# Two expert layers on one Trainium2 core: loop bodies of four tiles, four buffers of gathered rows, and a token table put in tile order

## The reference, cut to what matters

```python
router_logits = xt @ gate_w.T
routing_weights = jax.nn.softmax(router_logits, axis=-1)
top_w, top_idx = jax.lax.top_k(routing_weights, TOP_K)
full_w = jnp.zeros_like(routing_weights).at[rows, top_idx].set(top_w)
full_w = full_w / jnp.clip(full_w.sum(axis=-1, keepdims=True), 1e-09, None)
g = jax.nn.silu(jnp.einsum('th,ehi->eti', xt, w_gate))
u = jnp.einsum('th,ehi->eti', xt, w_up)
y = jnp.einsum('eti,eih->eth', g * u, w_down)
out = jnp.einsum('eth,te->th', y, full_w)
```

## Time and profile before

| | us |
|---|---|
| median of 3 runs | 1076.29 |
| lowest and highest run | 1075.6, 1079.83 |
| the profiled execution | 1073.37 |
| its span in the trace | 1071.6 |
| PE busy | 811.7 (76%) |
| DVE busy | 515.7 (48%) |
| ACT busy | 524.3 (49%) |
| POOL busy | 499.5 (47%) |
| mean granted TensorE clock | 0.908 |

### The profile page before, as it was taken

The page is one execution under the profiler, slowest core; times in us unless marked ns, Lnnn a source line. Parts: engine busy times, 40 slices in busy tenths (PEclk is TensorE's granted clock), DMA queues, the critical chain, the costliest instruction groups (busy, mean ns, idle before and its releaser), DMA issues.

```text
span 1071.6 us, 20434 instructions
## 1 busy us (share of the span) xinstructions
PE 811.7 (76%) x5206; PEld 441.1 (41%) x5207; DVE 515.7 (48%) x1523; ACT 524.3 (49%) x782; POOL 499.5 (47%) x413
## 2 busy tenths in 40 slices
PE   4998999997389993769871377878877778777770
PEld 3444455544244442335341243444444444444440
DVE  5653444564435533557763243544545435353432
ACT  5532334544356741345452165556756556555550
POOL 4880001001346755004575555566766556656560
PEclk9999999998589996979985698999999999989995
DMA  8553010000348958301110358878987878779668
GB/s 283 168 182 118 11 40 21 31 30 31 111 126 217 236 101 240 129 30 41 41 42 23 108 129 234 194 165 195 242 221 191 228 165 199 186 169 233 150 111 254
DMA packets 108391, 150.73 MB, mean 141 GB/s; under 512 B 18336, under 2 KB 59552, under 8 KB 108352
## 3 DMA queue, kind: packets, MB, share of 16 engines
q0 software_dynamic: 25760, 56.56, 26.9%
q1 hardware_dynamic: 80000, 93.49, 26.6%
q10 hardware_dynamic: 2592, 0.19, 0.2%
HBM read 107.34 MB, written 42.86 MB: 140 GB/s over the span
## 4 chain that ended last, share of the span: by engine, by line
PE 39%; DMA 15%; issue 14%; DVE 10%; DVEq 8%; ACT 5%; SPq 3%; POOL 3%; ACTq 2%; POOLq 0%; another core or an unknown queue 0%
PE pst L187 32%; DMA mid<-moe_normalised_rows,small 6%; DMA big<-in_L_ffn_w_down_dram 4%; DMA x_rows<-mid,small 3%; DVEq L1160 3%; DVEq L1154 2%; PE pst L1264 2%; PE pst L493 2%; POOL moe_tokens_of_experts L994 1%; DVE big L1146 1%; DMA big<-x_rows 1%; ACTq L1154 1%; DVE mid L1385 1%; DMA big<-in_L_ffn_wo_dram 1%; PE pst L953 1%
## 5 line engine op out<-in xcount | busy, mean ns | idle before, releaser
L187 PE MATMUL pst<-big,mid 128*128 (+1 forms) x1392 | 287.0, 359 | 22.1 <-DVE mid L1377 10.4
L1460 POOL DMA_INDIRECT x_rows<-mid,small x100 | 160.1, 1601 | 130.9 <-ACT mid L1321 77.0
L994 POOL DMA_INDIRECT moe_tokens_of_experts<-token_no,small x80 | 82.8, 1035 | 285.4 <-DVE small L1047 264.9
L187 PEld LDWEIGHTS pst<-big,mid 128*128 128x128 f16 x1392 | 137.8, 102 | 137.1 <-issue 47.6
L1450 POOL DMA_INDIRECT mid<-moe_normalised_rows,small x106 | 114.7, 1082 | 97.4 <-DVE small L1367 37.4
L1264 PE MATMUL pst<-big,mid 128*128 x520 | 132.3, 388 | 1.4 <-ACT mid L1313 0.9
L1302 ACT ACTIVATE mid<-pst 128x1024 f16<-128x1024 f16 x102 | 103.7, 1017 | 55.7 <-PE pst L1236 44.0
L1377 DVE SCALAR_TENSOR_TENSOR mid<-pst,small,mid 128x192 f32<-128x192 f32 (+1 forms) x100 | 42.6, 426 | 119.8 <-ACT mid L1308 87.8
L1236 PE MATMUL pst<-id,mid 128*128 128x128 f16 x816 | 66.5, 228 | 39.0 <-DMA mid<-moe_normalised_rows,small 34.5
L187 PE MATMUL pst<-ctxN,mid 128*128 128x512 f16 x384 | 88.6, 389 | 3.2 <-ACT mid L619 3.2
L1321 ACT ACTIVATE mid<-pst 128x512 f32<-128x512 f32 x100 | 59.9, 599 | 58.0 <-PE pst L1264 46.0
(11 more groups left out here) (201 smaller groups left out, 1193.4 us busy)
## 6 DMA issues: line engine op xcount, KB each, us to landing
big<-in_L_ffn_w_gate_dram SPq DMA_DIRECT2D x32, 384.0 KB
big<-in_L_ffn_w_up_dram SPq DMA_DIRECT2D x32, 384.0 KB
big<-in_L_ffn_wi_dram SPq DMA_DIRECT2D x16, 512.0 KB
big<-in_L_ffn_w_down_dram SPq DMA_DIRECT2D x32, 256.0 KB
big<-in_L_ffn_w_down_dram SPq DMA_DIRECT2D x64, 128.0 KB
moe_normalised_rows<-xn SPq DMA_DIRECT2D x18, 256.0 KB, 2.0
mid<-in_ctx_dram SPq DMA_DIRECT2D x16, 256.0 KB, 4.3
big<-in_ctx_turned_dram SPq DMA_DIRECT2D x16, 256.0 KB, 4.6
```

The source lines that it names most:

```text
L187: last = nc.tensor.matmul(dst, stationary(a, c), moving(b, c), start=(k == 0), stop=(k == 3 * len(parts) - 1))
L994: nc.gpsimd.indirect_dma_start(out=self.tab_d[:, :], out_offset=bass.IndirectOffsetOnAxis(ap=self.addr[j % 2][:, k:k + 1], axis=0), in_=to ...
L1460: nc.gpsimd.indirect_dma_start(out=acc_d[p][:, :], out_offset=bass.IndirectOffsetOnAxis(ap=self.si[p], axis=0), in_=self.y[p], in_offset=N ...
```

## The change

The loops take four tiles a turn. `experts` reads its numbers once per four tiles (5 values on DVE, ACT and POOL, 6 on PE), and `columns` is gone. In its place the whole table of row numbers is put in tile order once, before the loop: a 0/1 matrix `sel` has a one where table column c belongs to tile n; DVE casts the table to float16, PE transposes it, DVE copies it, PE multiplies by `sel` and adds the spare rows for tiles past the end, and DVE copies the result to `rows`, where tile t's row numbers are column t+2. There are four buffers `xg` and four index columns `gi`; the extra two buffers lie in `xT`. DVE makes h of t, splits it at once, copies the router weight of t+1, the row numbers of t+5, the rows to add to of t-2, and splits weights for the expert of t+2 last. The constants of the routing are made at the program's start, and the counts start from an earlier semaphore (`m_s` for `key_s`). The low part of the down weights in `moe1` is one subtraction of 128x1024 instead of two.

```diff
             def experts(self, eng, it, first, n):
                 _, values = nc.values_load_multi_w_load_instructions(
-                    self.etab[0:1, bass.ds(2 * it + first + 2, n)], engines=[eng.engine], min_val=0,
+                    self.etab[0:1, bass.ds(4 * it + first + 2, n)], engines=[eng.engine], min_val=0,
...
-            def columns(self, eng, it, first, n):
-                _, values = nc.values_load_multi_w_load_instructions(
-                    self.ctab[0:1, bass.ds(2 * it + first + 2, n)], engines=[eng.engine], min_val=0,
...
-            def dve_pair(self, dve, it, first):
-                e = self.experts(dve, it, 0, 3)
-                c = self.columns(dve, it, -2, 7)
-                for p in range(2):
-                    t = 2 * it + p
-                    self.rows_in_turn(dve, it + 1 + p, t + 3, 1 - p, c[5 + p])
-                    self.weights_in_turn(dve, it + 1 + p, t + 1, 1 - p, e[1 + p])
-                    if not (first and p == 0):
-                        self.h_high(dve, t - 1, 1 - p)
-                        self.h_low(dve, t - 1, 1 - p)
-                    with dve.If(e[p + 1] > e[p]):
-                        self.split_d_lo(dve, e[p + 1])
+            def dve_quad(self, dve, it, first):
+                e = self.experts(dve, it, 1, 5)
+                for q in range(4):
+                    t, p, g = 4 * it + q, q % 2, (q + 1) % 4
                     self.make_h(dve, t, p)
-                    if not first:
-                        self.rows_out(dve, it - 1, t - 2, p, c[p])
+                    self.h_high(dve, t, p)
+                    self.h_low(dve, t, p)
+                    self.weights_in_turn(dve, it + (2 if q == 3 else 1), t + 1, g, e[q])
+                    self.rows_in_turn(dve, t + 5, g)
+                    if not (first and q < 2):
+                        self.rows_out(dve, 2 * it + q // 2 - 1, t - 2, p)
+                    with dve.If(e[q + 1] > e[q]):
+                        self.split_d_lo(dve, e[q + 1])
...
+            def dve_rows(self, dve):
+                NE = self.NE
+                dve.wait_ge(self.tab_in, 32)
+                nc.vector.tensor_copy(self.tab16, self.tab).then_inc(self.rows_s, 1)
+                dve.wait_ge(self.route_pe, 5)
+                nc.vector.tensor_copy(self.tabT[0:self.CQ, :, :], bank16(3)[0:self.CQ, 0:self.NQ * P].rearrange("p (q s) -> p q s", q=self.NQ)).then_inc(self.rows_s, 1)
+                dve.wait_ge(self.route_pe, 6)
+                link(dve, nc.vector.tensor_copy(self.rows, bank(5)[:, 0:NE]))
...
-            def pool_pair(self, pool, it, first):
-                e = self.experts(pool, it, 1, 3)
-                for p in range(2):
-                    t = 2 * it + p
-                    self.gather(pool, t + 3, 1 - p)
+            def pool_quad(self, pool, it, first):
+                e = self.experts(pool, it, 1, 5)
+                for q in range(4):
+                    t, p = 4 * it + q, q % 2
+                    self.gather(pool, t + 5, (q + 1) % 4)
-                    with pool.If(e[p + 1] > e[p]):
-                        self.split_gu_lo(pool, e[p + 1])
+                    with pool.If(e[q + 1] > e[q]):
+                        self.split_gu_lo(pool, e[q + 1])
-                    if not first:
-                        self.scatter(pool, it - 1, t - 2, p)
+                    if not (first and q < 2):
+                        self.scatter(pool, 2 * it + q // 2 - 1, t - 2, p)
```

More of the change, by code:

```diff
@@ L882, in __init__ @@
                 self.r8 = small[:, 38:39]
-                self.gi = [small[:, 58 + q:59 + q].bitcast(I32) for q in range(2)]
+                self.gi = [row_no[:, q:q + 1] for q in range(4)]
                 self.si = [small[:, 60 + q:61 + q].bitcast(I32) for q in range(2)]
@@ L905, in __init__ @@
                 self.si_s = sem(f"{name}_rows_to_add_to")
-                self.xg_in = [sem(f"{name}_rows_gathered_{i}") for i in range(2)]
+                self.xg_in = [sem(f"{name}_rows_gathered_{i}") for i in range(4)]
                 self.x_full = sem(f"{name}_rows_transposed")
@@ L1183, in pe_route @@
             def pe_route(self, pe):
-                E = self.E
-                pe.wait_ge(self.key_s, self.b + NT)
+                E, NE = self.E, self.NE
+                pe.wait_ge(self.m_s, self.b + NT)
                 for t in range(NT):
-                    last = nc.tensor.matmul(bank(5)[0:E, 0:P], self.m16[:, t, :], ones16[:], start=(t == 0), stop=(t == NT - 1))
+                    last = nc.tensor.matmul(bank(4)[0:E, 0:1], self.m16[:, t, :], ones16[:, 0:1], start=(t == 0), stop=(t == NT - 1))
@@ L1189, in pe_route @@
                 last.then_inc(self.route_pe, 1)
                 pe.wait_ge(self.tab_s, 1)
[L1192 to L1194 removed]
+                nc.tensor.matmul(bank(3)[0:1, 12:12 + E], self.nt16, before16[0:E, 0:E], start=True, stop=True)
@@ new lines, in pe_route @@
+                nc.tensor.matmul(bank(4)[0:1, 192:192 + NE], self.nt16, self.past, start=True, stop=True).then_inc(self.route_pe, 1)
+                pe.wait_ge(self.tab_s, 3)
+                nc.tensor.matmul(bank(4)[:, 320:320 + NE], ones16[0:1, :], self.crow, start=True, stop=True).then_inc(self.route_pe, 1)
+                pe.wait_ge(self.rows_s, 1)
+                for q in range(self.NQ):
+                    last = nc.tensor.transpose(bank16(3)[0:self.CQ, q * P:(q + 1) * P], self.tab16[:, q * self.CQ:(q + 1) * self.CQ], id16[:])
@@ L1200, in act_route @@
+                last.then_inc(self.route_pe, 1)
+                pe.wait_ge(self.rows_s, 2)
+                for q in range(self.NQ):
+                    nc.tensor.matmul(bank(5)[:, 0:NE], self.tabT[0:self.CQ, q, :], self.sel[0:self.CQ, q, :], start=(q == 0), stop=False)
+                nc.tensor.matmul(bank(5)[:, 0:NE], spare16[:], self.over, start=False, stop=True).then_inc(self.route_pe, 1)
             def act_route(self, act):
@@ new lines, in dve_route @@
+                nc.vector.tensor_scalar(self.over, passed, E - 0.5, None, ALU.is_ge)
+                link(dve, nc.vector.scalar_tensor_tensor(self.colrow, earlier, -1.0, tile_row[0:1, :], ALU.mult, ALU.add))
+                link(dve, nc.vector.scalar_tensor_tensor(self.colrow, self.colrow, float(E), passed, ALU.mult, ALU.add))
+                nc.vector.scalar_tensor_tensor(self.crow, self.over, 4096.0, self.colrow, ALU.mult, ALU.add).then_inc(self.tab_s, 1)
+                dve.wait_ge(self.route_pe, 4)
@@ new lines, in dve_route @@
+                for q in range(self.NQ):
+                    nc.vector.tensor_scalar(self.sel[:, q, :], b4[:, 320:320 + NE], part_no[:, q:q + 1], None, ALU.is_equal)
+            def dve_rows(self, dve):
[6 more added lines that the diff above has]
+                link(dve, nc.vector.tensor_copy(self.rows, bank(5)[:, 0:NE]))
@@ L1321, in weigh, with act_quad @@
                 nc.scalar.activation(self.y[p], bank(6 + p), ACT.Copy).then_inc(self.y_s, 1)
[L1323 to L1327 removed]
+            def act_quad(self, act, it, first):
+                e = self.experts(act, it, 2, 5)
+                for q in range(4):
+                    t, p = 4 * it + q, q % 2
                     self.move_rows(act, t + 1, 1 - p)
                     self.silu(act, t, p)
[L1330 removed]
+                    if not (first and q == 0):
                         self.move_h(act, t - 1, 1 - p)
[L1332 to L1335 removed]
+                    if not (first and q < 2):
+                        self.weigh(act, 2 * it + q // 2 - 1, t - 2, p)
+                    with act.If(e[q + 1] > e[q]):
+                        self.split_hi(act, e[q + 1], self.first_tile(act, e[q + 1]))
             def act(self, act):
@@ L1446, in gather @@
+                self.dve_quad(dve, 0, True)
+                with dve.Fori(1, nq) as it:
+                    self.dve_quad(dve, it, False)
+                n = 4 * nq
+                self.rows_out(dve, 2 * nq - 1, n - 2, 0)
+                self.rows_out(dve, 2 * nq - 1, n - 1, 1)
+            def gather(self, pool, t, g):
                 pool.wait_ge(self.meta_s, t + 1 + self.CR)
-                pool.wait_ge(self.x_full, t - 1 + self.CR)
-                pool.wait_ge(self.wc_s, t - 1 + self.CR)
+                pool.wait_ge(self.x_full, t - 3 + self.CR)
+                pool.wait_ge(self.wc_s, t - 3 + self.CR)
```

270 lines of the change are left out of this document (123 added, 147 removed).

## The result

The changed kernel is **slower**: 1101.1 us (median of 4 runs, 1100.43 to 1107.07), where the kernel before took 1078.06 beside it (4 runs, 1075.6 to 1081.84). The ratio is 1.0223, 95% interval 1.0173 to 1.0272. The forecast was 1023, and its range ended at 1048.

The account below looks back on a forecast made before the run. The long expert loop was held by late DVE, DMA engines stopping the gain near 4.2 us per tile. Terms -48 - 2 - 4 + 1 = -53 took 1073.4 to 1020, 1023 as a median; range 1004 to 1048.

Parts of the forecast that it names:

- Order on DVE: Long loop: DVE's weight splits move from ahead of h of t to the tile's end; 8 us off.
- Four buffers: Long loop: a gather has four tiles' time to land, not two; 21 of PE's 25.6 us wait off.
- The rival: Scatters into one DRAM sum limit two tiles; long landings make the kernel slower, 1096, as a median 1099; chance 0.03.
- 1.45 + 1.08: Added to a scatter's landing: 1.45 us until the next on its sum, 1.08 for POOL's gather ahead of it.
- Gathers under 5: Sign of being right: PE's wait for gathers in the long loop falls from 26 to under 5 us.
- loads -33: Long loop: fewer register loads on DVE take 33 us off PE's 43.0 us wait before the transposes of h.
- Start of `moe1`: Long stage: first row numbers come 2 us earlier (ends: 4 off, 1 on), table put in tile order included.
- forecast 1 on: Short stage: table steps add 1.8 us, loads of some 0.6 move behind; 1 us on (0 to 3).
- The long and the short loop: Long: 62 us off, 14 given back to DMA, net 48 off; short: 4 off (0 to 9).
- the long loop at 4.2 us a tile: DMA engines' floor, 90 us off; as rival with all waits gone, 92 off, median 973, chance 0.07.
- half of the way from 1023 to 973: Lower end of the range, half of the way towards the rival where all waits go; given as 1004.
- What would show it: Signs listed for right or wrong: DMA share near 0.89 if right, 0.79 with tiles over 5 us if wrong.

Follow-up runs that it names:

- the control: The changed kernel with the expert number masked by one register operation ahead of each wait that uses it: 1105.57 us, ratio 1.0284.
- copies-first kernel: The changed kernel with DVE's copies of router weight, row numbers and rows to add to ahead of h: 1016.66 us, ratio 0.9594.
- best version: The changed kernel with four `y`, DVE's three small copies ahead of h, and POOL's weight split ahead of its gather: 988.0 us, ratio 0.9337.

## Why the prediction was wrong

**The step that failed** is "Order on DVE", with a false sentence under "Four buffers": "The row numbers of t+5 are copied where those of t+3 were." They are not; they stand behind h and its split, as the diff shows. The order counted what the split and h gain by standing first (8 us, of the 8.2 that gate and up waited for h, which are now 28.6), and never priced what was moved behind them: the copies of the router weight and of the row numbers. Before, the row numbers were copied at the start of a tile, and could be, for they need nothing of this tile. Now both copies wait for h, and so for PE's gate and up and ACT's silu (L1386 waits 118.7 us for ACT). The gather they serve has four tiles to spare, and I let that stand for the copy's cost. But POOL runs in order. Behind the gather stand the weight split and the scatter, and these two had little slack: a late scatter holds ACT, a late split holds PE and SP. A cheap step with slack was made the gate of two steps with little. The fall of 0.069 in the ratio from the control to the copies-first kernel (some 73 us) is the price, against a gain of 42 for the rest.

**The ring.** The rival had the place and the observable ("ACT's L1321 waits for scatters"), and I gave it 0.03. Two of its terms were too small. The landing, 5.3 us, came from the last two scatters on one sum. The chain of the changed kernel has eight scatters of the long loop before its last two, 6.84 to 7.54 us each; four of the ten (start us, us):

```profile
925.30 7.34 DMA x_rows<-mid,small
...
972.04 7.11 DMA x_rows<-mid,small
...
1067.50 5.07 DMA x_rows<-mid,small
...
1074.01 4.60 DMA x_rows<-mid,small
```

But a chain shows only the landings that something waited for. Read for all 78 scatters before the last two, from the trace's semaphore events, the landing (from the start of POOL's instruction) took 4.5 to 8.8 us with a mean of 6.2, against 4.5 to 9.3 and 5.8 in the kernel before. For about half of these scatters some of the 16 events are missing from the trace, so the figures may be a little low. And to 1.45 + 1.08 belongs the time that POOL's gather waits for its row numbers. The text of the rival says that it waits until h is made, but puts no time to it; it is 39.2 + 50.1 = 89.3 us over some 73 tiles, 2.4 us per two. Then the ring is, as an estimate, 6.2 + 2.5 + 2.4 = 11.1 us per two tiles, and the loop ran at 2 x 5.50 = 11.0, so the landing needed no 8.2 us to decide. That landings grew longer is not the cause by itself: they are as long or longer in the faster kernels, with a mean of 6.1 at 4.88 us per tile (copies first) and 6.5 at 4.47 (best version).

**The weights.** I wrote that SP's next load comes about a tile earlier, since DVE's split frees the slot. DVE's is not the last to free it there: POOL's ends at 869.69 and DVE's (L1160) at 868.19, and POOL stands behind the copies. The chain's ring of 16.95 us per three tiles is that.

**Terms that held.** DVE's idle time for "issue" ahead of its first work in a turn was to fall under 35 us: 31.3. Gathers under 5: 0.0, and with the copies first still none in the view. PE's wait for the split of h was to be about 10 and reads 0.0, but that is not the loads' doing alone: with the copies first, where PE isn't held earlier, it is 22.0 us over 340, so "loads -33" was too much. Start of `moe1`, forecast 2 us earlier: from the read of the table to the first copy it was 6.14 us in the earlier trace rows, and now

```profile
609.04 0.37 SPq L999 DMA_DIRECT2D mid<-moe_tokens_of_experts  x1
...
611.38 0.29 DVE L1236 CAST mid<-mid 128x256 f16<-128x256 int32 x1 [5.79 <-DMA mid<-moe_tokens_of_experts]
...
613.43 0.34 DVE L1370 COPY row_no<-mid 128x1 int32<-128x1 int32 x4
...
615.18 1.03 POOL L1451 DMA_INDIRECT mid<-moe_normalised_rows,row_no  x1 [4.60 <-issue]
```

613.43 - 609.04 = 4.39, so 1.75 earlier. The first gather follows the read by 6.14, where it was 7.38 before (604.99 - 597.61), so 1.2 of it arrives. The added steps take 613.43 - 611.38 = 2.05 us (forecast 1.8). In `moe0` the same stretch is 5.61 before and 5.60 now (forecast 1 on); there the read itself is issued at 277.05 and not at 279.86, 2.8 us earlier, for which the forecast had nothing. Which of the earlier steps gives that wasn't tested.

**Terms that were off in size.** The long and the short loop: -48 and -4 forecast, +16.9 and +12.6 measured. In the short loop (291 to 409 us) the same two waits show, 26.3 us of gathers for row numbers and 11.2 of ACT for scatters (10.4 for L1367 and 0.6 before, 296 to 399), while I had capped it at 0 to 9 us of gain and allowed no loss. The longer lead that the four buffers allow is worth some 64 us, not 21, in the kernel with the copies first; "loads -33" and "four buffers -21" look like one term, not two: without the lead, the rest of the change gives nothing (the lead without the rest wasn't tried). Two sums of the forecast don't come out either: the long loop at 4.2 us a tile is 90 us off in one place and 92 in another, and half of the way from 1023 to 973 is 998, not 1004.

**The DMA limit.** With the failed step undone the numbers come near the forecast: 4.88 us per tile at a share of 0.88, where it had 4.75 at 0.89, and the total is 42 us down where it had 53. That is in part luck: the terms have other sizes, the chain gives 40.4% to scatters, and opening two more paths (four `y`, POOL's split first) took the loop to 4.47 us, so 4.88 was not the DMA engines' limit. "What would show it" asked for 0.89 in the loop; the changed kernel had 0.73 with tiles of 5.50 us, which speaks for an engine's order and against the DMA engines. The best version runs at 4.47 us, with a share of 0.93 and 232 GB/s over 620 to 940 us, and stays above the 4.2 I had worked out as the floor. The Trainium skill, page "DMA: Bandwidth & Descriptors", section Specifications, gives about 358 GB/s of memory bandwidth per core. Nothing shown here comes near it: the highest are this 232 GB/s and the 239 of the earlier trace rows, with the engines busy 0.93 and 0.96.

## What to carry to other kernels

An instruction that is moved is priced by the engine queues of all who wait for it: ask what stands behind the waiting instruction in its own queue, and how much slack that has, not how much slack the waiting instruction has. A copy that waits for nothing belongs ahead of the work that does wait, however small the copy is and however late its result is due. A wait that reads zero after a change may only have moved to an earlier place on the same engine. And a buffer that is added and a stall that is removed may be one gain, so test each alone before adding them.

## What was unexpected of the hardware

The landing of one and the same kind of scatter, 128 rows, varies by a factor of two: 4.5 to 8.8 us in the changed kernel's long loop (mean 6.2; 23 of 78 under 5.3), 4.7 to 8.9 in the copies-first kernel. The last two of the changed kernel took 5.07 and 4.60 and those that its chain shows inside the loop 6.84 to 7.54, so neither a landing read at the end of a program nor one read from the chain is the mean landing of the loop.

DVE's cast of 128x128, 0.23 us at most places (875.49 in the timeline; the median of 80 is 0.227), took 0.99 beside POOL's weight split, and ended as the split did:

```profile
867.92 1.77 POOL L1151 TENSOR_TENSOR big<-big  x1
...
868.78 0.99 DVE L1394 CAST mid<-mid 128x128 f16<-128x128 f32 x1
```

At 885.49 it took 1.22 us, and there too its end (886.71) is that of POOL's split (884.87 + 1.75 = 886.62). Such casts are a small part of the time here (L1394 has a mean of 398 ns), but they stand in front of the row numbers when h comes first. The Trainium skill, page "SBUF — State Buffer", section "SBUF: two separate sides", says that GpSimd and VectorE, the latter in a 2-port performance mode or with two SBUF inputs, share a port pair that whichever starts first holds for its whole instruction. These two rows agree, for 868.78 + 0.99 = 869.77 and 867.92 + 1.77 = 869.69; that the cast runs in such a mode isn't shown by a row.
